# A compressed-interaction kernel: W0's pair sums on VectorE alone, W1 requested later from another queue, copies reordered

## The reference

```
for W, b in ((W0, b0), (W1, b1), (W2, b2)):
    z = einsum('bhd,bfd->bhfd', x_vec, x)            # 64x64, then 128x64 products per element
    x_vec = einsum('oc,bcd->bod', W, z) + b          # W0 is 128x4096, W1 and W2 128x8192
    outs.append(x_vec.sum(axis=2))
```

## Time and profile before

| what | us |
|---|---|
| median of 3 executions | 1118.36 (1117.12 to 1119.52) |
| the profiled execution: its own time | 1118.71 |
| the profiled execution: span from first to last instruction | 1117.0 |
| PE busy within the span | 1071.4 |
| VectorE, ScalarE, GpSimd busy | 857.4, 717.8, 867.2 |

### The profile page before, as it was taken

The page is one execution under the profiler, slowest core; times in us unless marked ns, Lnnn a source line. Parts: engine busy times, 40 slices in busy tenths (PEclk is TensorE's granted clock), DMA queues, the critical chain, the costliest instruction groups (busy, mean ns, idle before and its releaser), DMA issues.

```text
span 1117.0 us, 17733 instructions
## 1 busy us (share of the span) xinstructions
PE 1071.4 (96%) x4781; PEld 804.3 (72%) x4781; DVE 857.4 (77%) x2518; ACT 717.8 (64%) x2433; POOL 867.2 (78%) x727
## 2 busy tenths in 40 slices
PE   4879999999999999999999999999999999999997
PEld 3767677777768777777778777777777877777676
DVE  5565788878794787888885788888887588887982
ACT  4456676767673676767674576766766477676781
POOL 3456898988985789897977679797988579799560
PEclk9999999999999999999999999999999999999998
DMA  6752423223231231423332133333222232321000
GB/s 253 200 120 76 93 76 73 77 55 95 64 86 53 51 98 52 97 71 81 88 67 58 45 85 83 67 94 75 77 57 74 57 74 77 73 76 46 1 22 8
DMA packets 108325, 85.87 MB, mean 77 GB/s; under 512 B 71040, under 2 KB 73824, under 8 KB 108096
## 3 DMA queue, kind: packets, MB, share of 16 engines
q1 hardware_dynamic: 105680, 73.98, 27.4%
q10 hardware_dynamic: 2544, 10.75, 2.8%
HBM read 14.75 MB, written 0.79 MB: 14 GB/s over the span
## 4 chain that ended last, share of the span: by engine, by line
PE 84%; DVE 7%; ACT 5%; issue 2%; DMA 1%; POOL 1%; ACTq 0%; DVEq 0%
PE y L875 57%; PE l L895 10%; PE l L875 7%; PE xt L986 5%; DVE acc L762 3%; PE l2p L998 3%; ACT prod L650 2%; ACT y L639 1%; DVE bd L718 1%; DMA gram<-in_L_rec_W_dram 1%; DVE acc L747 1%; DVE x1l L728 1%; DVE gram L835 1%; PE l2p L975 1%; ACT x1h L548 0%
## 5 line engine op out<-in xcount | busy, mean ns | idle before, releaser
L762 DVE SCALAR_TENSOR_TENSOR acc<-y,x0t,acc 128x128 f32<-128x128 f32 x1792 | 493.2, 340 | 69.3 <-PE y L875 63.2
L650 ACT ACTIVATE prod<-y,x0t 128x128 f32<-128x128 f32 x1280 | 368.9, 381 | 232.7 <-PE y L875 225.8
L875 PE MATMUL y<-w1h,x1h 128*128 128x512 f32 x1024 | 466.5, 456 | 13.9 <-DVE acc L762 11.8
L875 PE MATMUL y<-w1h,x1l 128*128 128x512 f32 x1024 | 402.4, 393 | 0.0
L875 PE MATMUL y<-w1l,x1h 128*128 128x512 f32 x1024 | 401.2, 392 | 0.0
L441 POOL TENSOR_TENSOR z<-z,xg 128x512 f32<-128x512 f32 (+2 forms) x272 | 372.6, 1374 | 14.2 <-DMA z<-xg 13.9
L451 POOL TENSOR_TENSOR pacc<-pacc,prod 128x512 f32<-128x512 f32 x192 | 253.0, 1318 | 138.5 <-ACT prod L650 138.5
L875 PEld LDWEIGHTS y<-w1h,x1h 128*128 128x128 f32 x1024 | 193.4, 189 | 115.9 <-issue 45.7
L639 ACT ACTIVATE y<-y,x0t 128x128 f32<-128x128 f32 x768 | 215.9, 350 | 74.0 <-PE y L875 73.9
L747 DVE TENSOR_TENSOR acc<-y,acc 128x512 f32<-128x512 f32 x192 | 132.6, 691 | 136.7 <-ACT y L639 133.1
L875 PEld LDWEIGHTS y<-w1l,x1h 128*128 128x128 f32 x1024 | 193.1, 189 | 59.1 <-issue 29.1
(11 more groups left out here) (93 smaller groups left out, 664.2 us busy)
## 6 DMA issues: line engine op xcount, KB each, us to landing
z<-xg SPq DMA_DIRECT2D x480, 128.0 KB, 2.4
w2t<-in_L_rec_W_dram ACTq DMA_DIRECT2D x8, 512.0 KB, 12.3
gram<-in_L_rec_W_dram ACTq DMA_DIRECT2D x8, 512.0 KB, 4.4
xg<-in_r_input_dram SPq DMA_DIRECT2D x30, 128.0 KB, 3.9
z<-xg SPq DMA_DIRECT2D x32, 96.0 KB, 2.5
z<-xg SPq DMA_DIRECT2D x15, 192.0 KB
gram<-in_L_rec_W_dram ACTq DMA_DIRECT2D x1, 2048.0 KB, 10.3
out_dram<-z SPq DMA_DIRECT2D x4, 192.0 KB, 1.9
```

The lines of the kernel that those rows point to most:

```text
L650: last = nc.scalar.activation(prod[:, h % HSLOTS, k, :], y[c % YB][:, k * O:(k + 1) * O], ACT.Copy, scale=x0t[:, j, f:f + 1])
L762: ins = nc.vector.scalar_tensor_tensor(out=to, in0=of, scalar=x0t[:, j, f:f + 1], in1=b1r[:] if m == 0 else to, op0=ALU.mult, op1=ALU.add)
L875: ins = nc.tensor.matmul(to, stationary, moving, start=(first and k == 0), stop=(last and k == 2))
```

## The change

It has four parts.

1. The pair sums of W0 are made by VectorE alone and written directly into w0pair, with no w0sum, no copies by ACT and no share of GpSimd. For each eight shifts there are three additions of 8 x 32, 8 x 31 and 8 x 32 elements, both of whose inputs step by 65 floats. The first eight shifts also get a copy of the diagonal, and one addition of 96 elements ends the work. Each addition waits for the one before it (`pair_step`). w0pair moves from z into the end of the W2 buffer. GpSimd sets a strip of 2048 elements behind W0 to zero near the program's start.
2. The eight requests for W1 go from ACT's queue, where they stood directly behind W0's, to SP's queue, and wait until PE has transposed x.
3. On ACT, x1h of the first tile is made ahead of w1h of the first two blocks.
4. `LOWER_AFTER` is 2 instead of 3, so `lower` of the next group's first tiles is placed at e = 58. In group 0 `lower(0, LAST)` and the sum move from e = 15 to e = 14, and `left_lower(0)` moves ahead of the additions of the same e.

More of the change, by code:

```diff
@@ L72 @@
 TURN_AT = LAYER2_AT + CHUNKS
-LOWER_AFTER = 3
+LOWER_AFTER = 2
 ROWS_AT = (34, 40, 46)
 W2_AT = 14
+PAIR_SHIFTS = 8
 W1_AHEAD = 2
@@ L168, in cin_kernel @@
         xraw = zflat[0:GROUP_B, 0:2 * F * D]
-        w0raw, w0sum = w2raw[:, 0:F * F], w2raw[:, F * F:2 * F * F]
+        w0raw = w2raw[:, 0:F * F]
         zturned = zflat[:, ZSLOTS * GROUP - (ZT - 1) * P:]
@@ L196, in cin_kernel @@
         zturned_made = sem("zturned_made")
-        w0sum_made = sem("w0sum_made")
-        far_w0sum_made = sem("far_w0sum_made")
-        w0pair_made = sem("w0pair_made")
+        w0_spare_set = sem("w0_spare_set")
+        pair_step = sem("pair_step")
         w1_turned = sem("w1_turned")
@@ L399, in zin @@
             return zlater[t % LSLOTS] if n == 0 else z[:, zslot(t), :]
[L401 to L414, removed]
         @block.gpsimd
@@ L663, in _ @@
                     nc.scalar.copy(zleft[rows, EARLY], l2p[rows, i % 2, EARLY]).then_inc(early_left_made, 1)
-            act.wait_ge(w0sum_made, 3)
-            act.wait_ge(far_w0sum_made, 1)
-            for r in range(W0_STEPS):
[L667 to L672, removed]
-                nc.scalar.copy(to, near).then_inc(w0pair_made, 1)
             for r in range(W0_STEPS):
```

## The result

The changed kernel takes 1111.36 us (median of 5 runs, 1109.54 to 1112.90) against 1118.36 for the kernel before: a ratio of 0.9941, with a 95% interval of 0.9929 to 0.9953. That is faster by 0.6%, inside the predicted range. But the gain is 7.0 us (7.4 between the two profiled spans, 1117.0 and 1109.6) where 11.6 were forecast.

A forecast was written before the change was run, and what follows sets the result against it. PE, busy 1071 of 1117 us, was taken as the bound, so only its idling could shrink. Gains of 4.8, 2.4 and 4.4 sum to 11.6 us, from 1118.7 to 1107.1 us, range 1102.5 to 1112.5.

The forecast's parts named there:

- the three places: Where PE idles: W0's preparation up to 26.4 us, the end of group 0's first tile, and the later group ends.
- (b): Rival: group ends give nothing, since chunk 11 and bd are pushed as far as x1l was; 1111.5 us, chance 0.14.
- (d): Rival: W1 in a second ring takes half of W0's tail, W0 lands 3 us later; 1110.1 us, chance 0.05.
- early_layer0 earlier: Start of the kernel: W0's pair sums without ACT's copies let early_layer0 start at 21.6 us, gain 4.8 us.
- chunk 0 earlier, in all: First chunk: everything behind early_layer0 moves up by the same 4.8 us, if its inputs do.
- W1's requests: Start of the kernel: asking for W1 later from another ring costs 0, bounds 1 us earlier to 3 us later.
- x1h ahead of w1h: First tile on ACT: the new order changes nothing, 0, bounds 0.4 us either way.
- group 0: End of its first tile: earlier zleft gains 0.6, earlier x1l 1.96, less 0.2 for ACT's w2t copies; gain 2.4 us.
- group ends, 14 and the first: Moving x1l cuts PE's wait for chunk 12 by 0.53 us; 0.3 remains 14 times, plus 0.2 at group 0; gain 4.4.
- (c): Rival: VectorE additions with two stepping inputs cost 2.4 ns an element, 2.1 us more; 1109.2 us, chance 0.05.
- (e): Rival: PE's short bursts leave the granted clock low through the early stage; 35 us would give 1124.6; chance 0.03.
- (a): Rival: ACT's scaling does not hold PE back and each group end gives 0.53 us; 1103.5 us, chance 0.11.

The follow-up runs named there:

- e7: Changed kernel with x1h behind the two w1h on ScalarE, as before the change: 1111.57 us.
- e6: Changed kernel with left_lower and lower of group 0 back at their old places: 1111.86 us.
- e1: Changed kernel with LOWER_AFTER back at 3, nothing else: 1113.96 us.
- e2: Changed kernel with LOWER_AFTER = 0, so x1l stands ahead of chunk 9's addition: 1110.85 us.
- e3: Changed kernel with seven unread identity transposes behind each of the first three groups of W0 transposes: 1108.78 us.
- e9: Changed kernel with unread transposes: 7 behind each of the first three W0 turns, 16 before the first chunk, 24 and 6 in the tail: 1105.20 us.
- e4: Changed kernel with PE waiting for all of VectorE's pair sums before the first transpose of W0: 1111.89 us.
- e8: Kernel before the change with only the new W0 pair sums: 1115.83 us.
- e5: Changed kernel with W1's requests back on ScalarE's queue directly behind W0's: 1109.84 us.
- e11: Changed kernel run once more, unaltered, for a second profile: 1110.51 us.

## Why the prediction was right, and too large

The direction and the three places were right, and the time lies inside the range. But the range reached up to 1112.5 for the sake of rivals (b) and (d), which did not happen, and with 1 us for the clock and W0's landing, where the clock took 2.2 us at the start and the tail 0.6, and the landing gave 0.6 back by chance; two of the five executions (1112.77 and 1112.90) lie above it. That 1111.36 falls inside is partly luck.

The terms in the changed kernel's profile, us:
```
term                          predicted   measured
early_layer0 earlier             4.8        5.1   (0.6 of it W0's landing, by chance)
its 46 matmuls slower             -        -2.2
chunk 0 earlier, in all          4.8        2.8
W1's requests                    0          0     (mean of the landings)
x1h ahead of w1h                 0          0     (e7)
group 0                          2.4        1.5   (e6)
group ends, 14 and the first     4.4        3.6   (e1, e2)
tail                             -         -0.6
sum                             11.6        7.4
```
The small steps between the rows (0.1 from chunk 0 to chunk 12) belong to no term.

**W0's pair sums.** The step held up to the start of early_layer0, and failed at "Everything behind early_layer0 moves up by 4.8". The additions began 0.61 early. From there to early_layer0 it took 21.32 - 11.66 = 9.66 us against 9.33 forecast. The 256-element additions have a mean of 628 ns in place of 590, which is (628 - 150) / 256 = 1.87 ns an element where 1.72 was taken; two stepping inputs cost little more than one, and rival (c)'s 2.4 is refuted. The page of the Trainium skill that was named in the prediction has 1.76, for sources that hop 4 KiB, and 1.87 is nearer to that than to its 2.50. What was missing in the sum is the rate of the 46 matmuls behind it. Rival (e) had named the mechanism, "that leaves the clock low through the early stage", and set it aside because the bursts were more work than before. That was the wrong comparison. In the kernel before, PE also came from 8 us of idleness and was slow, but on W0's 16 transposes, in one piece just ahead of early_layer0:
```profile
21.88 3.83 PE L916 MATMUL y<-ident,z 128*128 128x128 f32 x16 [8.36 <-ACT z L673]
```
PE started 9 matmuls from 24 to 26 us, all of them transposes, and 34 in the 4 us behind them. In the changed kernel the transposes lie apart in PE's idle time, and early_layer0 is the first long work in one piece. By the pace of the matmuls PE was slow from 21.9 to about 25.5 us before, and is now from about 15.9 to 26.0, so the slow stretch grew longer and came to lie on early_layer0. That filling the gaps gives the 2.2 us back is shown (5.16 us in e3 and e9). That the order of the transposes is the reason is not: e4, with the order of the kernel before, still needed 6.05. Rival (e)'s size, 35 us of low clock, was far off: the longest in the early stage is 10 us, for 2.2 us of loss in the changed kernel.

**Group 0.** 1.5 in place of 2.4. Both waits went, but what was late next was sized too small twice. w1l of block 15 "gives back half" of zleft's gain: it gave back 0.97 of 1.02. And "less 0.2" for ACT's copies of w2t was 0.78, of the 2.19 won at x1l.

**Group ends.** Right in mechanism and place, and a fifth too large: 0.53 won at each, of which "only 0.3 remains"; it was 0.22 at fourteen of them. The 0.17 lost at chunk 4 was the forecast loss (0.23 there). The 0.13 by chunk 13 was not foreseen. bd ended 0.28 to 0.29 behind GpSimd's addition wherever it was put, which is what the prediction rested on, and speaks against rival (b). Rival (a), that all 0.53 stay, falls by the offsets; and moving x1l further ahead gives no more (e2).

**Tail.** No term stood for it, and none of the rivals. The 128 matmuls began 8.5 us earlier than before and took 17.40 in place of 16.20 us. The clock's low stretch came only 6 us earlier and lay almost whole on them; in the kernel before, part of it passed while PE waited:
```profile
1092.00:1096.00 4.00, 1.03 (x4) 0.70 0.00 0
1096.00:1100.00 4.00, 3.25 (x16) 0.50 0.00 0
```

**Still open.** What makes the low stretch at the first chunks come in nine of the fourteen profiles and not in four others that have the same wait of 1.9 us ahead of them (e1, e3, e4, e8) wasn't found. Of the runs without filling, e1, e4 and e8 are those whose 46 matmuls were slow for the shortest time (5.99 to 6.16 us, 6.62 to 7.34 in the others), but the kernel before, with 5.16, has the stretch. Not found either is why e4's early_layer0 is slow and that of the kernel before is not; nor who holds back chunks 8 to 13 of a group by 0.13; nor why W0's landing scatters with W1 on another queue. An earlier request of W0, or W2's copies at another place, weren't tried.

## What to carry to other kernels

When a step is pulled out of an engine's idle time, ask what that idle time or that filler did for the work behind it. Here TensorE's first work behind 8 us of idling ran at half rate in the kernel before and in e4, and behind waits of 1.9 us it did in some profiles and not in others. So let something worthless be that work: 21 unread transposes bought 1.4 us ahead of the first chunk here (e3, in spite of a later landing of W0; another 1.4 at the first chunks is not surely theirs, since some runs are spared that low stretch anyway), and 30 another 2.9 at the end. And read the rate off the matmuls (how many a microsecond), not off the granted clock alone.

A wait that is shortened at one place is worth what the next limit leaves. Read the offset between two profiles at each repeated unit, not the sum of the waits: the waits fell by 7.0 us and the time by 3.6.

## What was not expected of the hardware

- TensorE's rate behind idle stretches was halved even where the record of the granted clock says 1.00: 14 matmuls from 21 to 24 us in e5, against 22 in e9, whose row is
```profile
21.00:24.00 3.00, 2.38 (x22) 1.00 0.64 162
```
- The time for which it stays slow differs between runs of nearly the same program: the 46 matmuls took 5.99 us (e1), 6.05 (e4), 6.16 (e8), 6.67 (e5), 6.68 (e11) and 7.34 (the changed kernel).
- An addition of 256 elements on VectorE with both inputs stepping by 65 floats takes 628 ns. By the 1.72 ns an element of one such input it would be 590.
- A transfer of 2 MB whose neighbour is asked for on another queue landed anywhere in 1.5 us in ten profiles; behind each other on one queue, within 0.25 in four.
